# Attention block and routed feed-forward on one core: rows of the maxima moved to the end of the stacks and written on chip

## The reference

```python
Q, K, V = (proj(W_Q), proj(W_K), proj(W_V))              # 16 heads of 8 features
Q = _apply_rope(Q, cos, sin); K = _apply_rope(K, cos, sin)
scores = jnp.einsum('bhsd,bhtd->bhst', Q, K) / jnp.sqrt(jnp.float32(D_K))
scores = jnp.where(causal[None, None], scores, -jnp.inf)
attn = jax.nn.softmax(scores, axis=-1)
out = jnp.einsum('bhst,bhtd->bhsd', attn, V)
x = _layernorm(x + out_projected)
x = _layernorm(x + _ffn(x))      # softmax gate, top 2 of 8 experts, gelu, 128 -> 512 -> 128
```

## Time and profile before

| | |
|---|---|
| median of three runs | 849.88 us |
| the profiled execution: time / span | 844.29 / 842.5 us |
| mean granted TensorE clock | 0.898 of full |
| TensorE (PE) busy | 688.3 us, 82% of the span |
| VectorE (DVE) busy | 588.4 us, 70% |
| ScalarE (ACT) busy | 441.8 us, 52% |
| GpSimd (POOL) busy | 313.4 us, 37% |
| DMA | 83.67 MB, mean 99 GB/s |
| HBM written | 26.90 MB |

### The profile page before, as it was taken

One profiled execution on the slowest core, in us unless ns is written; L12 is line 12 of the kernel. 1 busy time (PEld: TensorE's weight loads), 2 busy tenths in 40 slices (PEclk: granted clock), 3 DMA queues, 4 the chain that ended last, 5 costly groups with the idle time before them and its releaser, 6 DMA issues.

```text
span 842.5 us, 18794 instructions
## 1 busy us (share of the span) xinstructions
PE 688.3 (82%) x5544; PEld 362.3 (43%) x5545; DVE 588.4 (70%) x1443; ACT 441.8 (52%) x840; POOL 313.4 (37%) x512
## 2 busy tenths in 40 slices
PE   5859999899989888898889898988769947899840
PEld 2343333333433333343333333432259937898730
DVE  6959788888898977689888789894416731223266
ACT  1340366766646555555556664656736713565524
POOL 3871222232131245412116523124723465444551
PEclk9985599999989988898989999899969977999985
DMA  8784423111010111101002011000167745687924
GB/s 304 252 276 149 142 68 109 45 46 32 15 47 2 46 52 34 55 9 45 18 30 68 28 48 46 1 2 16 33 167 203 212 120 147 172 225 210 294 86 117
DMA packets 68038, 83.67 MB, mean 99 GB/s; under 512 B 9314, under 2 KB 45672, under 8 KB 67824
## 3 DMA queue, kind: packets, MB, share of 16 engines
q1 hardware_dynamic: 63600, 74.04, 29.6%
q0 software_dynamic: 4352, 8.53, 2.9%
HBM read 55.77 MB, written 26.90 MB: 98 GB/s over the span
## 4 chain that ended last, share of the span: by engine, by line
PE 48%; DVE 23%; issue 11%; SPq 7%; ACT 4%; DMA 2%; another core or an unknown queue 2%; POOL 1%; DVEq 0%; ACTq 0%; POOLq 0%
PE banks L711 14%; DVE mx L1121 13%; PE banks L668 9%; PE banks L693 6%; PE banks L784 4%; PE banks L663 4%; PE banks L773 4%; PE banks L720 2%; SPq L567 2%; ACT region L829 2%; SPq L568 2%; SPq L561 1%; DMA region<-pairs 1%; DVE w_sb L908 1%
## 5 line engine op out<-in xcount | busy, mean ns | idle before, releaser
L1121 DVE TENSOR_REDUCE mx<-banks 128x1 f32<-128x512 f32 (+3 forms) x640 | 365.6, 630 | 57.9 <-PE banks L668 50.5
L829 ACT ACTIVATE region<-banks 128x1024 f32<-128x1024 f32 (+3 forms) x256 | 200.7, 837 | 147.2 <-PE banks L693 144.6
L668 PE MATMUL banks<-region 64*128 64x512 bf16 (+3 forms) x768 | 201.1, 360 | 12.7 <-DVE mx L1121 11.1
L693 PE MATMUL banks<-region 64*128 64x512 bf16 (+3 forms) x768 | 134.6, 347 | 17.6 <-ACT region L829 9.8
L711 PE MATMUL banks<-region 128*32 128x512 f32 (+3 forms) x1024 | 122.7, 553 | 3.2 <-POOL region L1365 3.1
L829 ACT ACTIVATE cs_sb<-banks 128x1024 f32<-128x1024 f32 (+2 forms) x128 | 90.3, 760 | 62.5 <-PE banks L693 57.7
L663 PE MATMUL banks<-mask_sb,half_sb 64*128 64x128 bf16 (+1 forms) x384 | 87.5, 255 | 36.3 <-DVE mx L1121 24.7
L1375 POOL DMA_INDIRECT results<-region,dest x72 | 71.9, 998 | 106.1 <-DVE region L1248 72.2
L1365 POOL TENSOR_SCALAR_AFFINE_SELECT region<-region 128x256 f32<-128x256 f32 x160 | 64.8, 412 | 98.0 <-ACT region L829 95.5
L784 PE MATMUL banks<-region,w1e 128*128 128x128 f32 x576 | 83.4, 292 | 19.2 <-ACT region L855 14.4
L1242 DVE TENSOR_TENSOR region<-banks,w1e 128x128 f32<-128x128 f32 x72 | 20.9, 291 | 111.8 <-PE banks L773 65.8
(11 more groups left out here) (176 smaller groups left out, 703.8 us busy)
## 6 DMA issues: line engine op xcount, KB each, us to landing
w1e<-in_w SPq DMA_DIRECT2D x72, 322.0 KB
region<-stack SPq DMA_DIRECT2D x128, 112.0 KB
stack<-x_sb SPq DMA_DIRECT2D x16, 384.0 KB, 3.3
region<-pairs SPq DMA_DIRECT2D x72, 66.0 KB
stack<-x_sb SPq DMA_DIRECT2D x16, 256.0 KB, 3.7
region<-results SPq DMA_DIRECT2D x8, 512.0 KB, 4.7
xT_sb<-in_xT SPq DMA_DIRECT2D x4, 512.0 KB, 12.2
stack<-fill SPq DMA_DIRECT2D x2, 1024.0 KB, 10.3
```

What stands on the lines that cost most here:

```text
L668: last = mm(ring[:, bank, m * n:(m + 1) * n], qst[rows, v % NG, slot_, sb_ * P:(sb_ + 1) * P], kst[rows, v % NG, slot_, t0:t0 + n], start= ...
L693: last = mm(score[:, slot_, par, 0:n], kst[rows, u % NG, slot_, j * P:(j + 1) * P], qst[rows, u % NG, slot_, s0:s0 + n], start=True, stop= ...
L829: nc.scalar.activation(probs[i % 6][:, :, 0:n], score[:, i % 2, :, 0:n], ACT.Exp, scale=SCALE).then_inc(exp_done, 1)
L1121: read(v.tensor_reduce(dst, src, AX.X, ALU.max, negate=True))
```

## The change

Blocks are renumbered so that the six blocks of parts are the first 48 rows, and the maxima's rows come behind them, at 48 to 50 of each half (`MROW = ROWS = 48`). `stack` in DRAM holds six blocks. Its fills and the wait for them go. Instead K's ones are written once, for all four unit buffers and both slots, by two DMAs from 3 partitions of a tensor `ones`. Each load brings 48 rows. The maximum pass multiplies 48 rows (`real`), since Q's rows 48 to 50 hold maxima of an earlier unit by then; the mask matmuls and the score matmuls keep 64 rows, and rows 51 to 63 are zero from the memset. TensorE waits once for the ones, ahead of the first unit.

```diff
-ROWS = 56
-MROW = 32
+ROWS = 48
+MROW = ROWS
-Q_PLACES = ((0, (0, 3, 6)), (1, (1, 2)), (2, (5,)))
-K_PLACES = ((0, (1, 3, 5)), (1, (0, 2)), (2, (6,)))
+Q_PLACES = ((0, (0, 1, 2)), (1, (3, 4)), (2, (5,)))
+K_PLACES = ((0, (1, 3, 5)), (1, (0, 4)), (2, (2,)))
...
-        fill = sb("fill", [P, 2, S], BF16)
+        ones = sb("ones", [P, S], BF16)
...
-                    sp.wait_ge(fill_set, 2)
-                    for w_ in range(2):
-                        sp.dma_start(stack[w_, :, MROW // 8].rearrange("b h r n -> (h r) b n"),
-                                     fill[:, w_:w_ + 1, :].broadcast_to([P, B, S])).then_inc(fills, 16)
...
+            sp.wait_ge(fill_set, 1)
             sp.wait_ge(stacks_clear, 1)
+            for par in (0, 1):
+                sp.dma_start(kst[64 * par + MROW:64 * par + MROW + 3, :, :, :].rearrange("p g s n -> p (g s) n"),
+                             ones[0:3, :].unsqueeze(1).broadcast_to([3, 2 * NG, S])).then_inc(fills, 16)
...
                 if c == 3:
-                    sp.wait_ge(fills, 16 * 2)
...
             pe.wait_ge(v_read, RING)
+            pe.wait_ge(fills, 32)
...
                     rows = slice(64 * par, 64 * par + 64)
+                    real = slice(64 * par, 64 * par + MROW)
...
-                        last = mm(ring[:, bank, m * n:(m + 1) * n], qst[rows, v % NG, slot_, sb_ * P:(sb_ + 1) * P],
-                                  kst[rows, v % NG, slot_, t0:t0 + n], start=(m == 0 and not is_masked),
+                        last = mm(ring[:, bank, m * n:(m + 1) * n], qst[real, v % NG, slot_, sb_ * P:(sb_ + 1) * P],
+                                  kst[real, v % NG, slot_, t0:t0 + n], start=(m == 0 and not is_masked),
...
-            pp.memset(fill[:, 0, :], 0.0).then_inc(fill_set, 1)
-            pp.memset(fill[:, 1, :], 1.0).then_inc(fill_set, 1)
+            pp.memset(ones[:, :], 1.0).then_inc(fill_set, 1)
```

## The result

The changed kernel is slower: 853.50 us median of 20 runs (848.83 to 857.31), the kernel before 844.53 of 20 on the same chips (834.61 to 852.90), ratio 1.0128, 95% interval 1.0104 to 1.0152. The ratio takes only the 13 of these 20 executions of before that lie within 1.5% of the fastest, with a median of 842.73 us, since longer ones count as a slower state of the chip. The medians of all twenty give 1.0106, and three repeats further down give 1.0094 to 1.0110. The three runs of before that stood ahead of the prediction were in the upper part of this spread. The profiled execution took 851.27 us with a span of 849.5, against 844.29 and 842.5.

A forecast was written before the change was run, and what follows sets the result against it. Bound by TensorE (48% of the chain) and VectorE (23%), the start by projection and rotation, then the DMA queue. Terms -0.2 + 0 + 0 + 0 + 0 gave 844.1 us profiled, 849.7 timed median; 8-in-10 range 846.2 to 854.5.

The forecast's parts named there:

- Maximum pass over 48 rows: Maximum pass matmuls and weight loads: rows hardly matter to their time, 0 taken, bounds -1.7 and +5.3 us.
- The rival by the clock: Main stretch, 100 to 600 us: fewer rows make clock falls more frequent, +6.5 us, 856.4; chance 0.14.
- a clock under 0.92 with the same gaps: Sign that the forecast is wrong, read from 100 to 600 us, where 0.93 to 0.95 was expected.
- the price per microsecond, 0.43: Cost of each microsecond at 1.2 GHz, from two stretches with the same work: 0.43 us.
- No fills: Start of the program: without the two fill stores the cosine table arrives sooner, -0.2 us taken, 0 to -0.6.
- the -0.6 end of the bound: Start of the program: most that the cosine table's transfer could gain without the fills, two microseconds of reduced traffic.
- Ones on chip: SP's queue at the start: two small added DMAs, 1.58 us of issue, fit in its slack, 0.
- Loads of 48 rows: First eight loads, before the chunk-4 store: same time with less data, 0 taken, bounds -1.0 and +0.4 us.
- Gaps: TensorE's unexplained 2.98 us standstill: one more gives 852.7, one less 846.7; chance 0.10 each.
- within 0.2%: Whole kernel: a difference under 1.7 us, which cannot be told from none; chance 0.48.
- slower: Whole kernel: slower by more than 0.2%, from the clock case and one more gap; chance 0.24.
- the clock's full case: Main stretch: a quarter more time at 1.2 GHz, +6.5 us, 856.4, outside the 8-in-10 range; chance 0.14.

The follow-up runs named there:

- s48: Changed kernel with each head's 48 rows side by side in DRAM, so a load is one piece; 1.0048 (1.0018 to 1.0078) against the kernel before.

## Why the prediction was wrong

*Maximum pass over 48 rows, "0".* This step failed. Its first half was right: a matmul and a weight load of 48 rows take what those of 64 take (351 for 350 ns, 94 for 94). The wrong half was to price rows by a matmul's duration alone and leave what they do to the clock to a rival of 0.14. The runs show the clock term: 64 rows put back give 0.9971, 48 rows in the kernel before give 1.0059 and 1.0080, and 56 and 40 rows fall in line. The prediction had named this as a sign of being wrong, a clock under 0.92 with the same gaps: it was 0.91.

*The rival by the clock, +6.5 us.* The mechanism, its sign and its place, the main stretch, were right, and its size came out low for the profile: falls grew by half (60 to 90 us at 1.2 GHz), not by the quarter that I had taken from the share of rows. By the price per microsecond, 0.43, the 30 us more are +12.9; the units show +11.2. In time the median moved 9.0 us, or 10.8 against the 842.73 that the ratio uses. The argument against it, that the clock stood at 0.50 in the first pass anyway, spoke only of that stretch: there VectorE was busy 33.71 us of 36 before and 34.05 after, and little could be lost. I should have weighed that 64-row matmuls had kept TensorE busy for 34.75 of 36 us without the clock coming back. That row can be read as a sign that such matmuls do little to hold the clock, though no run here tests it alone; and eight of the 15 slots of the main stretch had falls already.

*No fills, "-0.2".* The first projection started at 8.61 us for 9.26, which is the -0.6 end of the bound, but the 32 records behind it took 16.43 us for 15.57. The first stores went out at 19.64 for 19.49: nothing was left of it. SP had 8 us of slack before them in place of 4.

*Ones on chip, 0.* Right: 1.74 us of issue in idle time, no wait for them.

*Loads of 48 rows, 0.* Right: share 0.36, and 3.7 us of the cast come only with the other shape of s48, which uses more engines and is issued faster. But the share does not tell six engines from seven, as the prediction took it to: it was 0.36 for seven blocks as well, where seven of 16 would be 0.44. The rule of the Trainium skill quoted in the prediction (DMA: Bandwidth & Descriptors, "Why a DMA increments its semaphore by 16 and not by 1") fits both shapes: by it 6 of 16 engines carry a load of six blocks, 0.375 beside the measured 0.36, and all 16 carry one with 48 rows on both sides, beside 0.81 and 0.83. I used it only as a reason for "no gain", where it also pointed at the one edit of the load that pays.

*Gaps.* One of 3.07 us is in the chain after as one of 2.98 was before; that rival did not come about.

*The time.* 853.5 lies in the range of 846.2 to 854.5, but that is luck of the yardstick: the three runs shown of before had 849.88, twenty have 844.53. Against its own before the change is +1.28%, where "within 0.2%" had 0.48 and "slower" 0.24. The range of the difference should have been built from the ratio's rivals, with the clock's full case inside it.

## What to carry to other kernels

Where the granted clock falls now and then in the main stretch (0.94 here), cutting the rows of a matmul from 64 to 48 saved no time in it (351 for 350 ns) and lowered the clock. In a kernel like this, leave a half tile at its full rows, zeros and all, and save the bytes elsewhere. Price such a change by comparing equal stretches of the trace at both clock levels and multiply by how long the lower one may grow, and give that term the weight of the path it sits on. For loads, look at the share of the DMA engines while only they run: 0.36 here was a sign that the shape of the transfer sets the pace, and laying the source out in one piece was worth more than leaving rows away.

## What the runs showed of the hardware that was not expected

- Rows that multiply only zeros count for the granted clock: 1.0018 with 64 rows, 16 of them without effect on the result, and 1.0107 with 48 on the same chip; and in the kernel before, eight rows of zeros left out gave 1.0033 and a mean clock of 0.890 for 0.898.
- The effect is graded: 1.0033, 1.0059 to 1.0080 and 1.0100 for 56, 48 and 40 rows of 64.
- A fall of the clock in about the same place of the program took 3.4 us in the profile before and 6.8 in the one after, with TensorE busy through both.
- The issue of a DMA got cheaper with the shape of its source: 717 ns median for six blocks of eight rows, 422 ns for 48 rows in one piece, with the same 96 KB.
